# Cross-attention and expert block on one core: the row maximum as three bfloat16 words, split on GpSimd, with two stages of the tensor engine reordered

## The reference

```
q = layernorm(x) @ Wq;  k, v = split(ctx @ Wkv)        # 32 heads of 8
q, k = axial_rope(q, pos), axial_rope(k, pos)
logits = q . k / sqrt(8)                               # per head, 64 x 64
w = softmax(logits);  attn = w @ v
x = x + attn @ Wout + bout
scores = layernorm(x) @ Wg.T;  top 2 of 8 experts, softmax over the two
x = x + sum over the two: weight * W3[e] (silu(W1[e] h) * (W2[e] h)),  h = layernorm(x)
```

## Time and profile before

| what | us |
|---|---|
| median of 3 runs | 539.9 |
| the three runs | 539.9, 545.99, 537.12 |
| span of the profiled execution, first to last instruction | 535.6 |
| PE busy in that span | 475.5 |
| mean granted clock of PE | 0.967 of full speed |

### The profile page before, as it was taken

How to read it: one execution, slowest core, us unless ns; L and a number is a source line. 1 busy time by engine, 2 the same in 40 slices (tenths; PEclk the granted TensorE clock), 3 DMA queues, 4 the chain that set the end, 5 groups by cost and what they waited for, 6 DMA issues and landing times.

```text
span 535.6 us, 21711 instructions
## 1 busy us (share of the span) xinstructions
PE 475.5 (89%) x7701; PEld 366.7 (68%) x7701; DVE 404.8 (76%) x1199; ACT 350.6 (65%) x929; POOL 366.2 (68%) x634
## 2 busy tenths in 40 slices
PE   3675999999999999999999998798969999998790
PEld 2563676676667666666767665488969998897780
DVE  7476599898999999999998988765725556776663
ACT  3473777777787777778777786656636666665550
POOL 5243658888888888888888885338626555665651
PEclk9988999999999999999999998979979999999995
DMA  7910011111212122121211111233643446778844
GB/s 202 250 38 17 20 34 39 61 53 50 64 50 82 60 71 74 49 65 38 73 41 61 39 34 35 80 95 107 185 116 121 128 130 202 235 230 256 279 153 157
DMA packets 43226, 54.56 MB, mean 102 GB/s; under 512 B 6727, under 2 KB 36849, under 8 KB 43122
## 3 DMA queue, kind: packets, MB, share of 16 engines
q1 hardware_dynamic: 36642, 36.32, 24.4%
q0 software_dynamic: 6480, 16.85, 8.7%
HBM read 29.60 MB, written 23.94 MB: 100 GB/s over the span
## 4 chain that ended last, share of the span: by engine, by line
PE 64%; DVE 12%; issue 8%; DMA 7%; SPq 4%; POOL 3%; ACT 2%; POOLq 0%; DVEq 0%
PE logit_banks L1512 7%; PE bank L1368 6%; PE logit_banks L1328 6%; PE logit_banks L1309 5%; PE bank L1355 5%; PE qkv_banks L1277 5%; PE bank L1361 5%; PE logit_banks L1336 5%; PE logit_banks L1531 4%; DMA y_in<-result_rows 4%; PE qkv_banks L1288 3%; DVE negmax L741 3%; PE qkv_banks L1268 3%; PE bank L1298 3%; DMA xres<-in_L_ffn_W_dram 2%
## 5 line engine op out<-in xcount | busy, mean ns | idle before, releaser
L675 POOL DMA_INDIRECT result_rows<-blocks_io,blk_dest x71 | 72.5, 1022 | 64.4 <-ACT blocks_io L1223 35.9
L641 POOL DMA_INDIRECT routed_rows<-xs,slots x64 | 65.8, 1029 | 16.9 <-issue 16.9
L741 DVE TENSOR_REDUCE negmax<-logit_banks 128x16 f32<-128x1024 f32 x64 | 75.1, 1216 | 3.0 <-PE logit_banks L1309 3.0
L1121 ACT ACTIVATE late<-logit_banks 128x1024 f32<-128x1024 f32 x64 | 62.0, 1021 | 14.3 <-PE logit_banks L1336 14.3
L1006 DVE TENSOR_TENSOR gated<-xn,logit_banks 128x176 f32<-128x176 f32 x71 | 23.9, 336 | 53.9 <-ACT xn L1229 53.9
L648 POOL TENSOR_TENSOR ropes<-rope_a,ropes 128x512 f32<-128x512 f32 x32 | 41.3, 1290 | 28.3 <-DVE ropes L728 28.3
L748 DVE RECIPROCAL rden<-bank 128x256 f32<-128x256 f32 x32 | 55.9, 1746 | 2.1 <-PE bank L1361 2.1
L1512 PE MATMUL logit_banks<-w_hi,x_hi 128*128 x142 | 48.1, 339 | 9.4 <-issue 5.5
L1229 ACT ACTIVATE xn<-logit_banks 128x176 f32<-128x176 f32 x71 | 22.5, 317 | 49.2 <-PE logit_banks L1512 49.2
L632 POOL TENSOR_TENSOR mid<-mid,mask 128x512 f32<-128x512 f32 x44 | 44.7, 1035 | 12.1 <-ACT mid L1102 12.1
L1512 PE MATMUL logit_banks<-w_lo,x_hi 128*128 x142 | 46.2, 326 | 0.0
(11 more groups left out here) (219 smaller groups left out, 1367.1 us busy)
## 6 DMA issues: line engine op xcount, KB each, us to landing
blocks_io<-routed_rows SPq DMA_DIRECT2D x71, 129.0 KB
y_in<-result_rows SPq DMA_DIRECT2D x16, 512.0 KB, 4.7
x_sb<-in_x_dram SPq DMA_DIRECT2D x32, 128.0 KB, 2.1
out_dram<-o_sb SPq DMA_DIRECT2D x16, 256.0 KB, 5.3
ctx_sb<-in_ctx_dram SPq DMA_DIRECT2D x32, 64.0 KB, 2.1
blocks_io<-in_L_ffn_W_dram SPq DMA_DIRECT2D x4, 512.0 KB, 6.7
mid<-mT SPq DMA_DIRECT2D x128, 4.0 KB
routed_rows<-pad_row SPq DMA_DIRECT2D x15, 129.0 KB, 2.7
```

What stands on the lines that cost most here:

```text
L641: nc.gpsimd.indirect_dma_start(routed[:, :], bass.IndirectOffsetOnAxis(ap=slots[:, t.slot(TR), k:k + 1], axis=0), xs[:, t.slot(TR), k, :], ...
L675: nc.gpsimd.indirect_dma_start(results[:, :], bass.IndirectOffsetOnAxis(ap=blk_dest[:, b.slot(RB):b.slot(RB) + 1], axis=0), y_sb[:, b.slot ...
L741: V.tensor_reduce(negmax[:, t.par, 16 * half:16 * half + 16], ps_s[:, 1024 * half:1024 * half + 1024].rearrange("p (h k) -> p h k", k=N), ...
L1121: S.activation(pT[:, 1024 * half:1024 * half + 1024], ps_s[:, 1024 * half:1024 * half + 1024], ACT.Exp, scale=SCALE).then_inc(exp_done, 1)
```

## The change

The maximum is still taken by DVE, into the first of three parts of `negmax` (now 96 columns, laid out by row group, part and head). POOL computes two more parts (`split_max`, behind `pair` in its turn): part 1 is part 0 less its own upper 16 bits, part 2 is part 1 less its upper 16 bits. All three are transposed together (96 rows), copied and sent to three partitions of each row group, and the product reads only the upper 16 bits of each word as bfloat16, three rows against bfloat16 ones. PE's order becomes logits, attend, transpose_kq, project_v, shifted_logits, transpose_max, project_k, transpose_x, rank, project_out, project_q. ACT copies the values ahead of the exponentials and the transposed maximum between them. `project_k` waits for one more copy of values, `peak` for an earlier transposition, `transpose_max` for POOL's parts, and it repeats the waits that guard its bank; `ones_row` and its memset go.

```diff
--- before.py
+++ after.py
@@ -124,7 +124,7 @@
         ps_q, ps_a, ps_rank = ps_qkv[:, 0:D], ps_qkv[:, D:D + E], ps_qkv[:, D + E:D + 2 * E]
         last_ranks = ps_nd[:, D + E:D + 4 * E]
         ps_cnt = last_ranks[:, 2 * E:3 * E]
-        ps_mT = ps_qkv[0:HEADS, D + 2 * E:D + 2 * E + P]
+        ps_mT = ps_qkv[0:3 * HEADS, D + 2 * E:D + 2 * E + P]
         ps_half = ps_qkv[:, D + 2 * E + P:D + 3 * E + P]
         ps_k, ps_v = ps_qkv[:, 512:768], ps_qkv[:, 768:1024]
 
@@ -146,9 +146,8 @@
         std1 = sb("std1", [P, NPAIR])
         minus_half = sb("minus_half", [P, 2])
         rope_a = sb("rope_a", [P, 512])
-        negmax = sb("negmax", [P, 2, HEADS])
-        mT = sb("mT", [HEADS, 2, P])
-        ones_row = sb("ones_row", [P, N])
+        negmax = sb("negmax", [P, 2, 3 * HEADS])
+        mT = sb("mT", [3 * HEADS, 2, P])
         rden = sb("rden", [P, D])
         attnT = sb("attnT", [P, D])
         gate_x = sb("gate_x", [P, TR + 1, E])
@@ -267,6 +266,14 @@
         ms = mid[:, 2048:3072]
         rope_b, rot = ropes[:, 0], ropes[:, 1]
 
+        def maxima(par, part, r=slice(0, RG)):
+
+            return negmax[:, par].rearrange("p (r s h) -> p r s h", r=RG, s=3)[:, r, part]
+
+        def leading(par, part):
+
+            return negmax[:, par].bitcast(BF16).rearrange("p (r s h w) -> p r s h w", r=RG, s=3, w=2)[:, :, part, :, 1]
+
         x_hi = sb("x_hi", [P, 2, D], FR)
         x_lo = sb("x_lo", [P, 2, D], FR)
         h_hi = sb("h_hi", [P, 2, 2, P], FR)
@@ -300,6 +307,7 @@
         xT_done, xT_sb, qk_done, v_done, v_sb = (sem(s) for s in ("xT_done", "xT_sb", "qk_done", "v_done", "v_sb"))
         rope_done, rot_done = sem("rope_done"), sem("rot_done")
         kqT_done, kqT_sb, km_done, qm_done = (sem(s) for s in ("kqT_done", "kqT_sb", "km_done", "qm_done"))
+        parts_done, parts_step = sem("parts_done"), sem("parts_step")
         s_done, max_done, mT_done, mT_sb, ms_in, st_done, exp_done, pv_done = (
             sem(s) for s in ("s_done", "max_done", "mT_done", "mT_sb", "ms_in", "st_done", "exp_done", "pv_done"))
         gate_x_done, gate_done = sem("gate_x_done"), sem("gate_done")
@@ -330,7 +338,7 @@
         half_done, o_done = sem("half_done"), sem("o_done")
         o_stored = [sem(f"o_stored{n}") for n in range(4)]
 
-        N_POOL_CONST, N_DVE_CONST, N_W = 10, 11, 2
+        N_POOL_CONST, N_DVE_CONST, N_W = 10, 10, 2
         NW12 = E * KC
         NWT = NW12 + E
         wt_banks = [banks[0], banks[1], banks[2], banks[3]]
@@ -489,8 +497,8 @@
                 sp.wait_ge(mT_sb, t.n + 1)
                 wait_past(sp, st_done, t.times(2))
                 for r in range(RG):
-                    sp.dma_start(ms[32 * r:32 * r + 1, :].rearrange("a (g n) -> a g n", n=P),
-                                 mT[8 * r:8 * r + 8, t.par, :]).then_inc(ms_in, 16)
+                    sp.dma_start(ms[32 * r:32 * r + 3, :].rearrange("s (g n) -> s g n", n=P),
+                                 mT[24 * r:24 * r + 24, t.par, :]).then_inc(ms_in, 16)
 
             def body(do, t):
                 do(send_max, t.plus(1))
@@ -625,6 +633,15 @@
                 nc.gpsimd.tensor_tensor(xres[:, bass.ds(t.n, 1), :].rearrange("p a d -> p (a d)"),
                                         x_sb[:, t.par, :], bout_sb[:], ALU.add).then_inc(xb_done, 1)
 
+            def split_max(t):
+
+                pool.wait_ge(max_done, t.times(2, 2))
+                nc.gpsimd.tensor_tensor(maxima(t.par, 1), maxima(t.par, 0), leading(t.par, 0), ALU.subtract)\
+                    .then_inc(parts_step, 1)
+                pool.wait_ge(parts_step, t.n + 1)
+                nc.gpsimd.tensor_tensor(maxima(t.par, 2), maxima(t.par, 1), leading(t.par, 1), ALU.subtract)\
+                    .then_inc(parts_done, 1)
+
             def mask_keys(t):
                 pool.wait_ge(kqT_sb, t.n + 1)
                 wait_past(pool, s_done, t.n)
@@ -653,6 +670,7 @@
                 do(rotate, t.plus(2))
                 if t.plus(4).within(T) or t.plus(-2).within(T):
                     pair(t)
+                do(split_max, t.plus(1))
                 do(normalise_x, t.plus(4))
                 do(mask_keys, t.plus(2))
                 do(scatter, t.plus(-3))
@@ -737,9 +755,10 @@
             def peak(t):
 
                 dve.wait_ge(s_done, t.n + 1)
+                wait_past(dve, mT_done, t.n - 1)
                 for half in range(2):
-                    V.tensor_reduce(negmax[:, t.par, 16 * half:16 * half + 16],
-                                    ps_s[:, 1024 * half:1024 * half + 1024].rearrange("p (h k) -> p h k", k=N),
+                    V.tensor_reduce(maxima(t.par, 0, slice(2 * half, 2 * half + 2)),
+                                    ps_s[:, 1024 * half:1024 * half + 1024].rearrange("p (r h k) -> p r h k", r=2, k=N),
                                     AX_X, ALU.max, negate=True).then_inc(max_done, 1)
 
             def invert_sums(t):
@@ -824,7 +843,6 @@
                 ins.then_inc(dve_step, 1)
                 dve.wait_ge(dve_step, steps[0])
 
-            V.memset(ones_row[:], 1.0).then_inc(dve_const, 1)
             V.memset(vst, 0.0).then_inc(dve_const, 1)
             V.memset(seen[:], 0.0).then_inc(dve_const, 1)
             V.memset(w3_raw[:, :, :, H:HP], 0.0).then_inc(dve_const, 1)
@@ -1187,11 +1205,11 @@
                 if is_first(t, 1):
                     copy_weights(range(11, NWT))
                 do(copy_kqT, t.plus(2))
-                do(copy_mT, t.plus(1))
+                do(copy_v, t.plus(1))
                 do(normalise_x1, t.plus(-2))
                 do(exponential, t, 0)
+                do(copy_mT, t.plus(1))
                 do(exponential, t, 1)
-                do(copy_v, t.plus(1))
                 do(copy_xT, t.plus(4))
                 do(set_shares, t.plus(-2))
                 if is_first(t, 4):
@@ -1264,7 +1282,7 @@
             def project_k(t):
                 pe.wait_ge(xT_sb, t.n + 1)
                 wait_past(pe, rope_done, t.n)
-                wait_past(pe, v_sb, t.n - 2)
+                wait_past(pe, v_sb, t.n - 1)
                 M.matmul(ps_k, xT[:, t.slot(TR), D:D + P], wk_p[:], start=True, stop=True)
 
             def project_q(t):
@@ -1313,8 +1331,11 @@
 
             def transpose_max(t):
 
-                pe.wait_ge(max_done, t.times(2, 2))
+                pe.wait_ge(parts_done, t.n + 1)
                 wait_past(pe, mT_sb, t.n)
+                wait_past(pe, rank_read, t.n - 3)
+                pe.wait_ge(rope_done, upto(t.n + 2))
+                pe.wait_ge(gate_x_done, upto(t.n + 2))
                 M.transpose(ps_mT, negmax[:, t.par, :], ident[:]).then_inc(mT_done, 1)
 
             def shifted_logits(t):
@@ -1331,10 +1352,11 @@
                                      start=(b == 0), stop=False, skip_group_check=True)
                 pe.wait_ge(ms_in, t.times(16 * RG, 16 * RG))
                 for r in range(RG):
-                    row = slice(32 * r, 32 * r + 1)
+                    row = slice(32 * r, 32 * r + 3)
                     for c in range(KC):
-                        ins = M.matmul(banks[r][64 * c:64 * c + 64, :], ones_row[row, :],
-                                       ms[row, :].rearrange("p (g c k) -> p g c k", c=KC, k=N)[:, :, c, :],
+                        ins = M.matmul(banks[r][64 * c:64 * c + 64, :], ones_bf[row, 0:N],
+                                       ms[row, :].bitcast(BF16).rearrange("p (g c k w) -> p g c k w", c=KC, k=N, w=2)[
+                                           :, :, c, :, 1],
                                        start=False, stop=True, skip_group_check=True)
                     if r % 2:
                         ins.then_inc(st_done, 1)
@@ -1460,14 +1482,14 @@
                 do(attend, t.plus(-1), 1)
 
                 do(transpose_kq, t.plus(2))
+                do(project_v, t.plus(1))
+                do(shifted_logits, t)
                 do(transpose_max, t.plus(1))
-                do(shifted_logits, t)
+                do(project_k, t.plus(3))
+                do(transpose_x, t.plus(4))
                 do(rank, t.plus(-2))
-                do(project_k, t.plus(3))
-                do(project_v, t.plus(1))
                 do(project_out, t.plus(-1))
                 do(project_q, t.plus(3))
-                do(transpose_x, t.plus(4))
                 if is_first(t, 3):
                     pe.wait_ge(rope_tables, 1)
                     transpose_weights(range(0, 2))
```

## The result

| | median us | lowest to highest | runs |
|---|---|---|---|
| before | 539.25 | 537.12 to 545.99 | 4 |
| changed | 551.61 | 545.26 to 555.85 | 4 |

A forecast was written before the change was run, and what follows sets the result against it. PE bounded nearly every turn (9.34 us) before; the split makes POOL the bound at 9.46. +2.6 us over 22 turns, -1.3 in three without a scatter, -0.7 at the start: +0.6, forecast 540.5 us, range 531 to 550.

The forecast's parts named there:

- The product: PE's eight products of the maximum, fp32 to bfloat16: 0.86 to 0.22 us a turn, gain 0.64, bounds 0 and 0.83.
- The transposition of the maximum: On PE, moved behind the shifted logits: it waits less there, gain 0 to 0.2 us, taken as 0.2.
- The loop through DVE and PE: Normalised attention, projection and residual: closes in 8.92 us, so a gain of 0.42 us a turn at most.
- The split: Two added subtractions on POOL each turn, 0.26 us each: 0.60 us together, between 0.38 and 1.52, uncovered.
- The order on PE: PE's new sequence followed from POOL's beat: all hidden under POOL, rope ending at 9.0 us, less than 9.46.
- ACT: Busy 7.3 of 9.4 us, so copying values first is covered; the later maximum delays SP's transfers some 2.1 us.
- The three table turns "hidden": Three turns at 190 to 213 us where DVE writes the block table, 9.5 us: POOL's 9.46 is hidden there.
- The transfers: SP's four transfers of three rows for one: issue stays 0.67 us each, 1.4 us of room remain.
- The start: Values copied ahead of both exponentials at the start of the chain: -0.7 us.
- rival C: Words land late: issue grows from 0.67 to 1.9 us each, a loop of 11.2 us, 592 us; chance 0.04.
- Rival A: POOL isn't the bound, the split overlapping what is beside it: all turns 8.92 us, 527.4 us; chance 0.13.
- rival B: The split on POOL is dear, priced like the power: turns of 10.38 us, 564 us; chance 0.10.

The follow-up runs named there:

- old_order_no_split: Kernel before with the three-row bfloat16 product in its old order on PE and ACT, no split (parts 1 and 2 zero); 528.2 us, 0.984.
- one_word: Kernel before with one edit: the product reads only the leading 16 bits of the one-row maximum as bfloat16, no split; 525.5 us, 0.9776.
- new_order_no_split: Changed kernel without split_max on POOL, parts 1 and 2 of the maximum being zero; 555.16 us, 1.0367.
- the first experiment: Changed kernel with one call moved: ACT copies the transposed maximum ahead of the first exponential; 539.07 us, 1.0042.
- mt_before_x1: Changed kernel with ACT's copy of the transposed maximum ahead of both the residual's normalisation and the exponentials; 541.62 us, 1.0076.
- changed_third: Changed kernel unaltered, measured again in a third session; 548.85 us, 1.0224.
- mt_before_exp: Changed kernel with ACT's copy of the transposed maximum moved ahead of the first exponential; 539.07 us, 1.0042.
- mt_before_exp_no_split: Changed kernel with the maximum copied ahead of the exponentials and no split on POOL (parts 1 and 2 zero); 534.23 us, no ratio.
- x_on_scalar: Two kernels: the changed one with x normalised on ACT, the maximum copied ahead of the exponentials or of the residual's normalisation; 543.73 and 559.92 us.

## Where the prediction held and where it failed, step by step

The likeliest case was a change of less than 2%. The ratios are 1.0178 and 1.0224, and 1.02 lies inside both intervals, so that this case is neither confirmed nor refuted; both intervals lie above 1.009, where 540.5 for 539.9 is 1.001. The runs of 545.26 and 548.74 us fell inside the range, but by luck: its upper part stood for a split of up to 1.0 us on POOL, and the split took 0.5. The loss came by a way that the prediction had put at nothing, ACT's copy of the maximum.

- *The product*: 0.22 us forecast, 0.23 measured. Right, but a quarter of 0.86 was a guess between far bounds. The Trainium skill ("TensorE: Matmul & The Clock Gate", Back-to-back issue gap) gives 518 cycles for one product of 512 bfloat16 columns. The trace agrees if the eight, which go to eight separate pieces of the array, run side by side, since all eight together took what one would take by that figure; the prediction assumed this without saying so.
- *The transposition of the maximum*: PE doesn't wait for DVE or POOL, 0.24 in the chain. Right.
- *The loop through DVE and PE*, 8.92: the number is right, 8.94 in `old_order_no_split` and in `one_word`, and the chain there goes through DVE and PE alone. But POOL's own work is 8.92 in the same turns, so they don't tell the one bound from the other.
- *The split*: 0.60 us forecast for POOL, about 0.5 measured (9.37 - 8.86); each subtraction 0.24 for 0.26. A term slightly too large. The lengthening that the prediction weighed by the Trainium skill's rule on the SBUF interfaces that POOL shares with VectorE ("GPSIMD Engine Reference", Key points) isn't seen on the subtractions, 0.23 to 0.25 us in all 32 turns. It is seen the other way round, on DVE (under the table turns below).
- *POOL is the bound* of the changed kernel: wrong. It is with the copy ahead of the exponentials (9.33, 539.07 us, near the forecast of 540.5), and isn't in the kernel as changed (`new_order_no_split`: same turn without the split).
- *The order on PE*: I followed each stage from POOL's beat but let `rank` come with the attention's projection "from 5.45". What it waits for wasn't asked; `rank` starts 6.2 us after the rotation (165.21 - 159.01).
- *ACT*: this is the step that failed. "ACT has 7.3 of 9.4 us, so copying the values ahead of the exponentials is covered", and for the maximum only the delay of SP's transfers was counted. Both rest on a share of busy time. The maximum's copy frees a PSUM bank as well, and through `rank` and `project_q` PE waits for that each turn. The line that says so, `pe.wait_ge(mT_sb, ...)`, stands in the kernel before. Reckoned from rows of before: transposed keys copied 0.60, values 0.9, normalised residual 1.3, exponential 1.0, copy 0.26, and 5.6 of PE's chain make some 9.7 us, which could have been a rival on the slower side, at about 22 x 0.4 = 9 us.
- *The three table turns "hidden"* at 9.5: wrong. They are four, and dearer than POOL's beat. `place` waits for `rank`, so the delay comes on top of DVE's own work there: 10.3, 11.0, 10.1 and 10.0. Even at POOL's beat (the first experiment) they were 10.0, 9.9 and 9.8, so that cover was never there. Nor is it `rank` alone: in `mt_before_x1`, where nobody waits for `rank`, DVE works through the turn of 9.94 us without a wait, and against the 9.5 of before one instruction has grown, `seen` (L824, at 208.72: 0.73 us for 0.27). It starts while POOL masks the keys (207.39 to 209.42) and ends 0.03 us behind that; in 20 of that run's 26 turns from the first scatter on it lasts longer than 0.15 us and ends, like here, within 0.03 us of the end of a mask. In the changed kernel it starts behind the masks and takes 0.15.
- *The transfers*: four issues with three rows each took 2.96 us for 2.69, and nobody waits for their landing. Right, and rival C with it.
- *The start*, -0.7, and the turns without a scatter, -1.3: together -2.0 forecast, and -0.75 measured in `changed_third` (78.04 for 78.79). The turn ahead of the first scatter has 10.15 us where 8.92 was forecast, the two before it 8.2 and 8.7.

Rival A had the right turn (8.92) for a kernel without a split; rival B had the right side, with a wrong cause: the split wasn't dear.

## What to carry to other kernels

When a copy out of PSUM moves back in its engine's order, follow the semaphore of that copy to every stage that waits for it, those that only share the bank among them, and close the loop in microseconds; an engine that is busy 7.2 of 9.75 us can set the beat. Ask of a cheaper product whether it needs its precision at all: a number that cancels (softmax's shift) can be cut to the leading word, and the split, its wait and the new order fall away. When an order was changed to make room for an added step, measure the old order without that step: here it is worth 1.6% alone (0.984).

## What the runs showed that I had not expected

- A wait on several semaphores is put down to "issue" in the profile: 1.26 us in each turn, with the cause on another engine (165.00 to 165.21) and named only at 59.08, where one wait is left. An "issue" that stands far above those of the same instruction in other kernels is a question, not an answer.
- With 2.1 us of idle PE in a turn the granted clock fell to about 0.50 for 2 to 3.5 us in about every third turn, 0.93 over stretches of 50 us; with 1.26 us of idle time it stayed at 1.00.
- A small instruction of DVE can be held until POOL is through with a large one: `seen`, 128x8, takes 0.15 us by itself, and mostly 0.4 to 1.0 where it starts while POOL masks the keys (`mt_before_exp`, `mt_before_x1`). A new step on POOL shifts when the two meet.
- PE pauses of 0.4 to 1.2 us in the midst of its products with the ones (L1383, L1390 in the `x_on_scalar` kernels) appear in two or three turns each of `mt_before_exp`, `mt_before_exp_no_split`, `mt_before_x1` and both `x_on_scalar` kernels, always in the same turns, with 12, 6 or 9 products of the group left. They are put down to issue, and were not explained.
